# Cross-attention into a routed FFN: the half tile moved to the middle of a group, queries made in three stacked blocks, outputs divided before they are projected

## The reference

```python
# 16 batches of 256 tokens of width 128; a context of 1601 keys of width 96 for each; 16 heads of 64
def xattn(x, context, Wq, Wk, Wv, Wo, bo):
    q, k, v = x @ Wq, context @ Wk, context @ Wv          # split into 16 heads
    attn = softmax(einsum('bhid,bhjd->bhij', q, k) * 64 ** -0.5)
    return einsum('bhij,bhjd->bhid', attn, v) @ Wo + bo   # heads put side by side
x = x + xattn(layernorm(x), ctx_768, Wq, Wk, Wv, Wo, bo)
x = x + ffn(layernorm(x), ...)    # sigmoid router in 4 groups, 4 of 32 experts of width 64, and a shared one
```

## Time and profile before

| | before |
|---|---|
| median of 3 runs | 3226.2 us (3225.82 to 3226.91) |
| the profiled execution's own time | 3223.51 us |
| its span, first to last instruction | 3221.7 us |
| TensorE busy | 3179.9 us (99%) |
| VectorE busy | 2389.6 us (74%) |
| ScalarE busy | 2017.8 us (63%) |
| GpSimd busy | 1333.2 us (41%) |
| mean granted TensorE clock | 0.997 of full speed |

### The profile page before, as it was taken

How to read it: one execution, slowest core, us unless ns; L and a number is a source line. 1 busy time by engine, 2 the same in 40 slices (tenths; PEclk the granted TensorE clock), 3 DMA queues, 4 the chain that set the end, 5 groups by cost and what they waited for, 6 DMA issues and landing times.

```text
span 3221.7 us, 40836 instructions
## 1 busy us (share of the span) xinstructions
PE 3179.9 (99%) x15118; PEld 2534.7 (79%) x15118; DVE 2389.6 (74%) x4882; ACT 2017.8 (63%) x2356; POOL 1333.2 (41%) x894
## 2 busy tenths in 40 slices
PE   7999999999999999999999999999999999999999
PEld 5777777778777777778777777777877778777787
DVE  5777777777777777777777777777777777777766
ACT  4666666666666666666666666666666666676555
POOL 5333443334333343334443344333433334225566
PEclk8999999999999999999999999999999999999999
DMA  2000000000000000000000000000000000105553
GB/s 82 1 17 1 17 1 1 18 1 18 1 18 1 18 1 1 17 1 18 1 18 1 18 1 18 1 1 18 1 18 1 18 1 1 40 3 122 120 129 76
DMA packets 31707, 67.48 MB, mean 21 GB/s; under 512 B 8339, under 2 KB 9620, under 8 KB 31124
## 3 DMA queue, kind: packets, MB, share of 16 engines
q1 hardware_dynamic: 31508, 64.88, 7.8%
HBM read 61.72 MB, written 2.62 MB: 20 GB/s over the span
## 4 chain that ended last, share of the span: by engine, by line
PE 96%; DVE 1%; POOL 1%; issue 1%; ACT 0%; DMA 0%; POOLq 0%; SPq 0%; DVEq 0%; ACTq 0%
PE st L593 12%; PE st L596 12%; PE side L535 11%; PE op L606 11%; PE op L612 11%; PE st L599 11%; PE op L609 11%; PE side L629 3%; PE st L716 2%; PE st L718 2%; PE st L717 2%; PE side L528 1%; PE op L620 1%; PE op L623 1%; PE side L530 1%; PE side L529 1%
## 5 line engine op out<-in xcount | busy, mean ns | idle before, releaser
L473 POOL TENSOR_TENSOR p_lo<-p_full,p_hi 128x1024 fp32r<-128x1024 f32 x320 | 819.7, 2562 | 1753.1 <-ACT p_hi L877 1753.1
L1156 DVE TENSOR_REDUCE m_part<-side 128x1 f32<-128x400 f32 x2016 | 1072.7, 568 | 502.3 <-PE side L535 502.2
L874 ACT ACTIVATE p_full<-st 128x1024 f32<-128x1024 f32 x768 | 788.8, 1027 | 876.8 <-PE st L599 848.5
L877 ACT ACTIVATE p_hi<-st 128x1024 fp32r<-128x1024 f32 x768 | 784.9, 1022 | 0.0
L1139 DVE TENSOR_TENSOR p_lo<-p_full,p_hi 128x1024 fp32r<-128x1024 f32 x448 | 545.5, 1218 | 85.6 <-ACT p_hi L877 85.6
L535 PE MATMUL side<-cT_hi,qT_hi 96*128 96x400 f32 x2016 | 554.5, 346 | 0.0
L593 PE MATMUL st<-qT_hi,cT_hi 97*128 97x512 f32 x1664 | 540.8, 406 | 11.9 <-DMA qT_hi<-m_row 11.1
L596 PE MATMUL st<-qT_lo,cT_hi 96*128 96x512 f32 x1664 | 524.3, 396 | 0.0
L606 PE MATMUL op<-p_hi,v_hi 128*97 128x512 f32 x1536 | 487.6, 398 | 1.6 <-DVE p_lo L1139 1.6
L612 PE MATMUL op<-p_hi,v_lo 128*97 128x512 f32 x1536 | 480.4, 394 | 0.0
L609 PE MATMUL op<-p_lo,v_hi 128*97 128x512 f32 x1536 | 480.4, 394 | 0.0
(11 more groups left out here) (171 smaller groups left out, 3072.1 us busy)
## 6 DMA issues: line engine op xcount, KB each, us to landing
w_rep<-w_rows SPq DMA_DIRECT2D x64, 512.0 KB, 6.6
keys_nat<-in_ctx_keys SPq DMA_DIRECT2D x16, 672.0 KB, 6.0
keys_tur<-in_ctx_turned SPq DMA_DIRECT2D x16, 600.4 KB, 4.8
gud_raw<-in_moe_w SPq DMA_DIRECT2D x2, 1152.0 KB, 7.7
out_x<-x SPq DMA_DIRECT2D x8, 256.0 KB, 2.0
x<-in_x SPq DMA_DIRECT2D x1, 1920.0 KB, 12.7
qT_hi<-m_row SPq DMA_DIRECT2D x64, 4.0 KB
oT<-e_row SPq DMA_DIRECT2D x64, 4.0 KB
```

The source lines that it names most:

```text
L473: pool.tensor_tensor(p_lo[:, slot(s), :], p_full[:, s % 2, :], p_hi[:, slot(s), :].bitcast(F32), ALU.subtract).then_inc(s_lo_pool, 1)
L874: act.activation(p_full[0:m, s % 2, :], made, ACT.Exp, scale=SCALE)
L877: act.activation(p_hi[0:m, slot(s), :], made, ACT.Exp, scale=SCALE).then_inc(s_ex, 1)
L1156: dve.tensor_reduce(m_part[:, k % NT, k // NT:k // NT + 1], where[:, 0:MAXW], AX.X, ALU.max).then_inc(s_drain, 1)
```

## The change

1. **Half tile in the middle.** Step 6 is now the half tile (`HALF`), steps 7 to 12 are tiles 6 to 11, and `st` and `p_full` alternate over the group's edge, (n + s) % 2, since a group has an odd number of steps. `scores` of step 1 of the next group now waits for exp(12).
2. **Stacked queries.** Four heads of 96 rows are made as three blocks of 128: heads 0 to 2 fill rows 0 to 95, and head 3's rows lie in three pieces of 32 on rows 96 to 127. A Q job 0 has two blocks (six matmuls), Q job 1 has one (three). ScalarE and VectorE then copy each job out in three and two pieces (`unstacked`).
3. **Divided before projection.** Y and its row of last-key exponentials are gone. A transfer brings the denominators out of `oT` as 8 x 128; VectorE adds the last key's and inverts them in step 4 of the next group; a transfer stores them, and another spreads them over 96 partitions (`r_rep`). VectorE divides in step 10 (`divide_first`, 96 x 768) and step 11 (`divide_last`, three pieces of 32 x 256), ScalarE makes the high part ahead of exp(12) (`divided_hi`), and VectorE the low part (`divided_lo`). One job Z projects all four heads as three blocks (nine matmuls of 256 columns), and VectorE adds the result up over the batch in `y_sum`; once in a batch, job V turns it and adds it to `x1`.
4. **Places.** M jobs are 4, 3, 4, 3, 3, 4, 4, 4, 3 in steps 2 to 10 (before 3, 3, 4, 3, 4, 4, 3, 4, 4). T is the only job of step 11. Step 12 has Q0 before the weighing of step 10, Z behind it, and Q1 behind the weighing of step 11. `late_steps` runs behind lo(0) of the next group, `early_steps` at the end of the group, and part of the layer norm's statistics in step 11 (`batch_stats`).
5. **The last batch** is projected in chunk 1, and its routing is done in chunk 2.

```diff
-        PLACES = {2: ("MM", "M"), 3: ("MM", "M"), 4: ("MM", "MM"), 5: ("MM", "M"), 6: ("MM", "MM"),
-                  7: ("MM", "MM"), 8: ("MM", "MY"), 9: ("MM", "MM"), 10: ("MM", "MM"), 11: ("YY", "YT"),
-                  12: ("QQ", "")}
-        EXTRA = {1: {5: "U"}, 2: {5: "L", 3: "N"}, 3: {5: "R"}}
+        PLACES = {2: ("MM", "MM"), 3: ("MM", "M"), 4: ("MM", "MM"), 5: ("MM", "M"), 6: ("MM", "M"),
+                  7: ("MM", "MM"), 8: ("MM", "MM"), 9: ("MM", "MM"), 10: ("MM", "M"), 11: ("", "T"),
+                  12: ("Q", "Z", "Q")}
+        EXTRA = {1: {3: "V", 5: "U"}, 2: {5: "L", 3: "N"}, 3: {5: "R"}}
...
             def project_queries(where, g, half, k):
-                for h in range(2):
-                    head = g * GH + 2 * k + h
-                    o = where[0:DC, h * NQ:(h + 1) * NQ]
-                    pe.matmul(o, A_hi[:, head, :], x_hi[:, half, :], start=True, stop=False)
+                for block in ((0, 1), (2,))[k]:
+                    o = where[:, block % 2 * NQ:(block % 2 + 1) * NQ]
+                    pe.matmul(o, A_hi[:, g, block, :], x_hi[:, half, :], start=True, stop=False)
...
-            def project_head(where, head, at):
-                for q in range(2):
-                    mm = pe.matmul(where[:, q * YW:(q + 1) * YW], oT[:, at + q * P:at + (q + 1) * P],
-                                   B_all[:, head, :], start=True, stop=True)
+            def project_outputs(where, g):
+                pe.wait_ge(s_ol, g + 1)
...
+                for k in range(3):
+                    pe.matmul(where[:, 0:NQ], B_hi[:, i, k, :], o_hi[:, k, :], start=(k == 0), stop=False)
+                    pe.matmul(where[:, 0:NQ], B_lo[:, i, k, :], o_hi[:, k, :], start=False, stop=False)
+                    mm = pe.matmul(where[:, 0:NQ], B_hi[:, i, k, :], o_lo[:, k, :], start=False, stop=(k == 2))
...
                 pv(S - 2)
...
+                side_jobs(at[S - 1][2])
                 pe.wait_ge(s_ml, 16 * (g + 2))
-                pe.wait_ge(s_sum, g + 1)
+                pe.wait_ge(s_ex, n + (S - 1))
...
+                scores(n + S, 0, (i + 1) % 2, next_par)
+                pe.wait_ge(s_ex, n + S)
+                scores(n + S, 1, (i + 1) % 2, next_par)
                 pv(S - 1)
...
+        def unstacked(tile, where, k):
+            last = slice(3 * NQ, GQ)
+            if k == 0:
+                return [(tile[0:DC, 0:BANK], where[0:DC, :]),
+                        (tile[0:DT, last], where[DC:P, 0:NQ]),
+                        (tile[DT:2 * DT, last], where[DC:P, NQ:BANK])]
+            return [(tile[0:DC, BANK:3 * NQ], where[0:DC, 0:NQ]),
+                    (tile[2 * DT:DC, last], where[DC:P, 0:NQ])]
...
+            def invert_denominators(g):
+                dve.wait_ge(s_dl, 16 * (g + 1))
+                dve.wait_ge(s_el, g + 1)
+                dve.tensor_tensor(den[:, :], den[:, :], e_row[:, g % 2, :], ALU.add).then_inc(s_rc, 1)
+                dve.wait_ge(s_rc, 2 * g + 1)
+                dve.reciprocal(den[:, :], den[:, :]).then_inc(s_rc, 1)
...
+            def divide_first(g):
+                dve.wait_ge(s_rr, 16 * (g + 1))
+                dve.tensor_tensor(o_all[0:DC, :, :].rearrange("p k t -> p (k t)"), oT[0:DC, 0:3 * NQ],
+                                  r_rep[:, 0:3 * NQ], ALU.mult)
...
+            def divide_last(g):
+                for k in range(3):
+                    third = slice(k * DT, (k + 1) * DT)
+                    ins = dve.tensor_tensor(o_all[DC:P, k, :], oT[third, 3 * NQ:GQ], r_rep[third, 3 * NQ:GQ], ALU.mult)
+                ins.then_inc(s_on, 1)
...
 # ScalarE, in a group
-                for s in range(1, FULL):
+                for s in range(1, S):
+                    if s == HALF:
+                        low_half()
+                    if s == S - 1 and g:
+                        divided_hi(g - 1, jobs_at(g - 1)["Z"][0] + 1 if g > 1 else 0)
                     exp(s)
...
-                low_half()
+                if g < NG - 1:
+                    keep_last(g + 1, place["T"][0] + 1)
                 for k, j in enumerate(place["Q"]):
                     queries_hi(bank(j), j + 1, k, i % 2)
-                exp(FULL)
-                if g < NG - 1:
-                    keep_last(g + 1, place["T"][0] + 1)
...
 # VectorE, in a group
                 lo(0)
+                if g:
+                    late_steps(g - 1)
                 for t in range(2, S):
+                    if g and t == 4:
+                        invert_denominators(g - 1)
                     if t == S - 1:
+                        if g:
+                            divided_lo(g - 1)
+                        lo(t - 1)
+                        lo(t)
+                        side_jobs(at[t][0])
+                    elif t == HALF:
+                        side_jobs(at[t][0])
+                        lo(t - 1)
                         sum_half()
-                        side_jobs(at[t][0])
-                        early_steps()
-                        lo(t)
                     elif t == S - 2:
                         lo(t - 1)
+                        if g:
+                            divide_last(g - 1)
                         side_jobs(at[t][0])
                     else:
                         side_jobs(at[t][0])
                         lo(t - 1)
                     side_jobs(at[t][1])
+                    if g and t == S - 3:
+                        divide_first(g - 1)
...
+                side_jobs(at[S - 1][2])
+                early_steps()
```

More of the change, by code:

```diff
@@ L587, in _, with scores @@
             turn_maxima(bank(J0_T))
-            def scores(s, slot, par):
-                keys = slice(s * P, s * P + P)
+            def scores(n, s, slot, par):
+                tile = tile_of(s)
+                keys = slice(tile * P, tile * P + P)
                 halves = [slice(j * BANK, (j + 1) * BANK) for j in range(2)]
+                into = st[:, (n + s) % 2]
                 for j in range(2):
-                    pe.matmul(st[:, s % 2, j, :], cT_hi[par][:, keys], qT_hi[slot][:, halves[j]],
-                              start=True, stop=False)
+                    pe.matmul(into[:, j, :], cT_hi[par][:, keys], qT_hi[slot][:, halves[j]], start=True, stop=False)
                 for j in range(2):
-                    mm = pe.matmul(st[:, s % 2, j, :], cT_hi[par][0:DC, keys], qT_lo[slot][:, halves[j]],
-                                   start=False, stop=(s == FULL))
-                for j in range(2 if s < FULL else 0):
-                    mm = pe.matmul(st[:, s % 2, j, :], cT_lo[par][:, keys], qT_hi[slot][0:DC, halves[j]],
+                    mm = pe.matmul(into[:, j, :], cT_hi[par][0:DC, keys], qT_lo[slot][:, halves[j]],
+                                   start=False, stop=(s == HALF))
+                for j in range(0 if s == HALF else 2):
+                    mm = pe.matmul(into[:, j, :], cT_lo[par][:, keys], qT_hi[slot][0:DC, halves[j]],
                                    start=False, stop=True)
@@ L707, in _ @@
             pe.wait_ge(s_ml, 16)
[L708 removed]
+            scores(0, 0, 0, 0)
             pe.wait_ge(s_Ap, 3)
[L710 removed]
+            scores(0, 1, 0, 0)
             turns(body)
@@ L798, in queries_hi @@
                 act.wait_ge(s_fill, filled)
-                act.activation(qT_hi[slot][0:DC, k * BANK:(k + 1) * BANK], where[0:DC, :], ACT.Copy).then_inc(s_qh, 1)
-            def products(banks, cols):
-                return banks[:, :, cols].rearrange("p j (c m) -> p j c m", c=2)
-            def four_heads(tile, n):
-                return tile[:, 4 * n:4 * n + 4, :].rearrange("p (c j) m -> p j c m", c=2)
+                for into, made in unstacked(qT_hi[slot], where, k):
+                    ins = act.activation(into, made, ACT.Copy)
+                ins.then_inc(s_qh, 1)
             def keep_products(n, banks):
@@ L1000, in queries_lo @@
                 dve.wait_ge(s_qh, count)
-                cols = slice(k * BANK, (k + 1) * BANK)
-                dve.tensor_tensor(qT_lo[slot][:, cols], where[0:DC, :], qT_hi[slot][0:DC, cols].bitcast(F32),
-                                  ALU.subtract).then_inc(s_drain, 1)
+                high = unstacked(qT_hi[slot], where, k)
+                for (into, made), (kept, _) in zip(unstacked(qT_lo[slot], where, k), high):
+                    ins = dve.tensor_tensor(into, made, kept.bitcast(F32), ALU.subtract)
+                ins.then_inc(s_drain, 1)
             def combine_max():
@@ new lines, in divided_lo, with add_outputs @@
+            def divided_lo(g):
+                dve.wait_ge(s_oh, g + 1)
+                dve.tensor_tensor(o_lo[:, :, :], o_all[:, :, :], o_hi[:, :, :].bitcast(F32),
+                                  ALU.subtract).then_inc(s_ol, 1)
+            def add_outputs(where, filled, g):
+                dve.wait_ge(s_fill, filled)
+                if g % NGB:
+                    dve.tensor_tensor(y_sum[:, :], where[:, 0:NQ], y_sum[:, :], ALU.add).then_inc(s_drain, 1)
```

(3 more changed lines are left out.)

370 lines of the change are left out of this document (219 added, 151 removed).

## The result

| | before | after |
|---|---|---|
| median | 3226.0 us (4 runs, 3223.3 to 3226.9) | 3523.3 us (4 runs, 3522.0 to 3525.4) |
| ratio, 95% interval | | 1.0923 [1.0906, 1.0941] |
| mean length of a group, from the first and last `keep_output` | (2920.7 - 90.3) / 63 = 44.9 us | (3219.3 - 95.4) / 63 = 49.6 us |

The prediction was 3209 us, range 3170 to 3240. The result lies 283 us above that range. What follows the last `keep_output` takes 3223.5 - 2920.7 = 303 us before and 3525.4 - 3219.3 = 306 after, so the loss is in the groups: 4.7 us in each on average.

The account below looks back on a forecast made before the run. TensorE's work was taken to bound the groups. -78.7 us of TensorE work, +50.0 Q1 wait, +12.6 in steps 2 and 3 and -1.1 once only gave -17.2 on a median of 3226.2: 3209.0 us, range 3170 to 3240.

Parts of the forecast that it names:

- What lies under cover: Work priced at no group time: step 4's inverting (1.3 us on VectorE), the transfers, the maxima row and the half tile.
- a long wait of Z for o_lo: Sign listed as showing the forecast wrong: in step 12, Z waiting long for the divided output's low part; no size given.
- rival 3: Slower: small VectorE and ScalarE pieces cost more than their columns; 3252 us at 100 ns more each; chance 0.15.
- The Q1 wait: Step 12: Q1 waits until VectorE empties Q0's bank, 9.66 against TensorE's 8.84 us: 0.82 us, 61 times, 50.0 us.
- rival 4: Waits eat what the work saves, to within 0.2%: a mean Q1 wait of 1.0 to 1.2 us; chance 0.13.
- Pieces don't overlap: VectorE pieces starting on other partitions run one after another; taken for `divide_last` and Q0's low part, giving 0.82 us at Q1.
- rival 1: Small pieces overlap on VectorE, so Q1 waits only 0.42 us: -42 us, 3184 us; chance 0.2.
- rival 2: No wait at Q1 at all, ScalarE or VectorE reaching their work earlier than counted: -67 us, 3159 us; chance 0.1.
- Steps 2 and 3: Step 3's second M waits for VectorE to empty step 2's fourth M: 0.1 or 0.3 us, 63 x 0.2 = 12.6 us.
- The half tile in the middle: Step 6: its chain low_half, sum_half, exp, lo starts 0.93 us in, weighing comes 7.2 later; counted as covered.
- The edges: Costs paid once: start +1.5 us, group 0's reductions +2.2, waits gone at the last groups' ends -4.8; net -1.1.
- The forecast of TensorE's work: TensorE in the groups: 149.6 us of work and waits removed, 70.9 added for Z and V, net 78.7 us less.

Follow-up runs that it names:

- nothing held: The changed kernel with `divide_last` moved to step 10, the denominators' addition on GpSimd and lo(11) on VectorE: 3278.3 us, 1.0164.
- last version: nothing held, plus Q0 copied out ahead of exp(12) and lo(12), M jobs moved from step 2 to 10 and 7 to 6, `late_steps` at group's end: 3197.8 us.
- both edits: The changed kernel with `divide_last` moved to step 10 behind `divide_first` and the denominators' addition moved to GpSimd ahead of lo(3): 3312.6 us, 1.0269.

## Why the prediction was wrong

**The step that failed** is the price of VectorE's two-input work: "the add 0.28" under "What lies under cover", and "`divide_last` three times 0.42" in the path to Q1. Both were taken from columns alone, and both instructions read two tensors from SBUF while GpSimd subtracts. They cost 1.77 us and 3 x 1.115 = 3.35 us instead (two pieces at 0.42 and the third at 2.53). The cover that I named for step 4 was short by that: 1.49 us more in a step where I had counted four reductions without lo, and the M jobs waited (taking the addition away gave 75 us). The late division held up `o_hi`, `o_lo` and with them Z, the sign that the prediction had listed as "a long wait of Z for o_lo"; it was worth 134 us by its own move and 140 us by GpSimd's. Together the runs take 245 us off the 297 by which the change is slower (3523.3 to 3278.3), with these two instructions back at their columns' price. They include the time that TensorE ran at its lower level. Its weighings alone are 0.51 us a group longer in the changed kernel than with nothing held (table below), some 32 us; the rest of the clock's share isn't separated.

**The sentence that excluded it** was rival 3's: small pieces cost more than their columns, "against it: nothing in the rows depends on partitions". That was true and beside the point. The direction of rival 3 was right, its mechanism was not: the price doesn't depend on the piece but on who runs on GpSimd at that moment. Here 3523 is also far beyond its 3252. The sign was in the kernel before. Its line L1125, in the expert part, subtracts with two SBUF inputs (min/median/max in ns):

```profile
L1125 DVE TENSOR_TENSOR gud_lo<-gud_raw,gud_hi x17: 544/551/2777, 2885.2 to 2908.5; 128x384 fp32r<-128x384 f32 x17
```

One form, a median of 551 and a maximum of 2777: five times its price with nothing of its own to explain it. Four of the 17 began beside a running GpSimd subtraction, and they alone are longer (676 to 2777 ns), each ending 0.41 to 0.42 us behind it. The kernel before hides its own rule well: VectorE's lo is in even steps and GpSimd's in odd ones, and from 100 to 2850 us all that VectorE begins beside a `p_lo` of GpSimd are reductions, work with an input in PSUM and a small memset.

**Where the group's time went.** In the traces I charged each matmul with the time from the end of the one ahead to its own end, so that a wait counts for the job that waited, and took the mean of 60 groups (from `keep_output` of group 1 to that of group 61). The forecast's column is the kernel before with the prediction's terms put in.

| us a group | before | forecast | changed | lo(11) on VectorE | nothing held | three M in step 2 | last version |
|---|---|---|---|---|---|---|---|
| scores | 17.71 | 17.67 | 17.69 | 17.69 | 17.69 | 17.68 | 17.68 |
| weighings | 17.64 | 17.64 | 18.15 | 17.63 | 17.64 | 17.64 | 17.71 |
| M | 5.88 | 6.08 | 8.03 | 8.02 | 6.77 | 6.47 | 6.20 |
| Y, or Z | 1.79 | 1.05 | 3.44 | 1.20 | 1.14 | 1.22 | 1.22 |
| Q | 1.60 | 1.89 | 1.80 | 2.38 | 1.97 | 1.09 | 1.09 |
| all others | 0.37 | 0.42 | 0.42 | 0.42 | 0.42 | 0.42 | 0.42 |
| group | 44.99 | 44.75 | 49.53 | 47.34 | 45.64 | 44.52 | 44.32 |

**The other steps, one by one:**
- *The Q1 wait*: the mechanism was right, the size wasn't. With the lo(11) edit, in the forecast's own order of work, Q takes 2.38 - 1.09 = 1.29 us a group more than without the wait, where 0.82 was forecast: 79 us in 61 groups, not 50. At one group's end of that trace TensorE's path comes to 8.88 us (forecast 8.84) and the one over VectorE to `o_hi` to 4.14 (4.1), but the reduction starts 0.20 us behind TensorE's scores 11, which the sum had set at the same time, ScalarE's three pieces take 1.35 instead of 1.2, and some 0.1 lies in what follows them. The mean is nearer to rival 4's 1.0 to 1.2 us than to the sum's. That the wait with nothing held, 0.88 us, lies so near 0.82 is luck: the divisions had been moved ahead there, and for that order my own working gave 0.35.
- *Pieces don't overlap*: the three pieces of `o_all` are written to the same partitions and read from others. Where GpSimd doesn't hold them (both edits, chain of the same stretch as above) they stand 0.43 us apart for 0.42:

```profile
1567.92 0.42 DVE o_all L1124
1568.34 0.01 issue
1568.35 0.40 DVE o_all L1124
```

  The wait is thus there for reads as well as for the write of the earlier trace rows. So what the Trainium skill states (VectorE: DVE Perf Modes, Two Vector instructions with no wait between them), and the prediction weighed, holds here in both forms, and rival 1 (3184) falls, as does rival 2 (3159).
- *Steps 2 and 3*: 0.2 us a group forecast. The fourth to sixth M of a group stand 0.51 us over their price with nothing held; three M in step 2 took 0.27 of it away, 16.8 us. The prediction's 2.89 + 1.15 + 1.07 is 5.11, not 5.14, which changes little.
- *The half tile in the middle* was priced at nothing, and costs a wait. On ScalarE, exp(6) waits for `sum_half` (92.6 us in 64 groups of the changed kernel), so lo(6) is late, and it stands ahead of the reductions that free the side banks. With nothing held:

```profile
1584.81 1.22 DVE L1256 TENSOR_TENSOR p_hi<-p_full,p_hi 64x1024 fp32r<-64x1024 f32 x1
...
1586.06 2.23 DVE L1273 TENSOR_REDUCE m_part<-side 128x1 f32<-128x400 f32 x4
...
1586.85 0.77 PE L599 MATMUL side<-cT_hi,qT_hi 96*128 96x400 f32 x2
```

  Elsewhere such a pair of M is recorded at 0.53. The second M of step 8 is 0.23 us late in every group, 14 us in all; with one M less in step 7 it is the fourth that is late, by 0.12. In step 6 the first two M are together 0.16 us late in the mean, in three of a batch's four groups; no run tests why.
- *Sizes*: the 8x128 reciprocal 0.94 (forecast 0.95), `divide_first` 0.99 (0.95), `o_hi` 0.84 (0.84). The spread of 384 KB lands after 3.2 us. Z takes 1.14 (1.05).
- *The edges*: -1.1 was forecast. `keep_output` of group 0 comes at 95.4 instead of 90.3, 5.1 later for my 1.5; behind it the reductions of group 0 let TensorE wait 4.3 us for a `p_lo` where it waited 1.6 (2.2 forecast for them). The 4.8 us at the last groups' ends didn't come: from the last but one `keep_output` to the last one it takes 39.8 us in the last version and 39.5 before. What follows is 3.3 us longer in the changed kernel.

**The forecast of TensorE's work**, -78.7 us, comes out but for some 8: with the Q1 wait gone and nothing held, scores, Z, Q and all others are together 0.12 us a group above the forecast's. With all waits of the prediction taken away too (three M in step 2), the sum would be -17.2 - 50.0 - 12.6 = -79.8; measured is -17.3, and that this is nearly the forecast's -17.2 is chance. What is missing in between are the M jobs, 6.47 instead of 5.88 (35 us over 60 groups), Z (10), and some 16 at the edges and in the three groups outside the mean. VectorE is busy for 2278 of 2700 us in the last version, 84% against the 75% of the earlier trace rows, partly because lo(11) had to move to it. That the M jobs would stop waiting if it had less to do is argued, not shown: moving work out of its way gave 10 us in two steps.

## What to carry to other kernels

Before putting a VectorE instruction with two SBUF inputs, a copy or a `tensor_scalar` from SBUF into a step, look at what GpSimd does in that step, and price it at the rest of GpSimd's instruction if they meet; reductions and work with a PSUM input are free to lie there (beside GpSimd's `p_lo` the kernel before has 855 reductions from PSUM at 560 to 578 ns and 183 updates of `x` from PSUM at 340 to 352, the same as elsewhere). A line whose maximum is several times its median, with one shape, is worth a look in the timeline before any new work is priced by its column count. When one held instruction is moved, follow the ones behind it: here the collision passed from the division to `o_lo`, and then the wait from Z to Q1.

## What I had not expected of the hardware

- An instruction of 8x128 elements can take 2.0 us instead of 0.27, until 0.14 us behind the end of GpSimd's; a copy 1.62 (0.21 free) and a `tensor_scalar` 1.46. A reduction of the same size takes 0.26 in any case. A held instruction with two SBUF inputs ends behind GpSimd's by its own price less some 0.14 us: 0.14 for one of 0.27, 0.28 for 0.42, 0.41 for 0.55, 0.81 for 0.95.
- The order of start decides: a piece of `divide_last` that began 0.13 us ahead of GpSimd took 0.42, the next one 2.54. GpSimd's subtraction takes in turn 3.07 instead of 2.38 when a `p_lo` of VectorE that began first runs for another 0.8.
- TensorE, after its wait of 1.88 us ahead of Z, was granted 0.87 and then 0.56 of its clock in two stretches of 3 us, and took 0.85 instead of 0.465 us for a pair. With waits of 1.1 us in the same place the run's mean clock was 0.995.
